# Layer-1 feed-forward, first pass: row statistics taken in the attention before it, normalization moved to ScalarE's tanh and VectorE, weight preparation cut into pieces

## The chip, the cores and the metric

The kernel runs on one core of a Trainium2 chip. Its engines are TensorE (PE; its weight loads are listed as PEld), VectorE (DVE), ScalarE (ACT), GpSimd (POOL) and the queue that issues most DMAs (SP). The metric is the device time of one execution in microseconds.

## The reference

Two layers, each a graph attention and a feed-forward, on 2708 rows of 256 values, in float32. What the change touches is the end of the second attention and the second feed-forward:

```python
def _L1_gnn_ref(x, adj_matrix, attn_mask, Wqkv, bqkv, Wout, bout, graph_bias):
    ...
    attn = jax.nn.softmax(scores, axis=-1)
    out = jnp.einsum('hnm,hmd->hnd', attn, vh)
    out = out.transpose(1, 0, 2).reshape(n, d)
    return out @ Wout + bout

def _L1_ffn_ref(x, ln_w, ln_b, W, b):
    def step(h, _):
        h = h + 0.01 * jnp.tanh(h)
        h = h * jax.nn.sigmoid(h)
        h = _layernorm(h, ln_w, ln_b)
        h = jnp.einsum('bsc,dc->bsd', h, W) + b
        return (h, None)
    x, _ = jax.lax.scan(step, x, None, length=30)
    return x
...
x = x + _L1_gnn_ref(_layernorm(x, axis=-1), adj, adj, ...)
x = x + _L1_ffn_ref((_layernorm(x, axis=-1))[None], ...)[0]
```

So the feed-forward starts with a layer norm of x (no weight, no bias), and then runs 30 iterations of blend, silu, layer norm and a 256x256 product.

## The kernel before

**Tiles and pairs.** The rows lie in 22 tiles of 128 (`NT`), two to a pair, so 11 pairs (`NPAIR`), in `X` of [128, 22, 256]. `BATCHES` groups the pairs for the small arithmetic on row statistics: pairs 0 to 2, 3 to 5, 6 to 8, and 9 to 10. Every stage is a `Phase` with a block in which each engine has its own program, written out by hand in order; semaphores join them, and a barrier of all engines ends the phase.

**Layer-1 attention** (`layer1_attention`, names `a_...`). Its steps run per tile (i, b) and pair of heads hp. In each such step PE turns the exponentials of two heads in three chunks c, DVE and ACT copy the turned blocks out of PSUM (L1075), DVE adds the bias and takes maxima of scores of later heads (L1160, L1165), ACT takes exponentials of later heads (L1124), and PE multiplies with V (L1301). In step hp = 0, chunk 1, `project` (L1206 on DVE) adds the projected output of the tile before to `X`; the last tile's stands alone at the end. POOL adds the adjacency bias (L1101) and the output bias to X (L1105), and has nothing more to do once the last tile's are done. The first and the last pair of tiles are written out, the nine between them are a hardware loop.

**Layer-1 feed-forward** (`layer1_ffn`, names `f_...`).

- *The first normalization.* DVE takes `bn_stats` of all 22 tiles of X in four hardware loops, with the moments of each batch behind them (`slot_moments`, L143 and L94 to L101). POOL turns each batch's moments into an inverse deviation and a shift (`slot_deviation`, `inverse_deviation`, L109 to L114: add, multiply, power, multiply), then writes the normalized rows to `gg` (`standard_rows`, L119), one instruction per tile.
- *The weights.* Four DMAs bring W, its bias, ln_w and ln_b. PE turns W (L2192), ACT copies it out (L2143), DVE scales it and makes two helper matrices (L2080 to L2084), PE multiplies these (L2198, L2202), DVE folds the biases and the mean in (L2088 to L2093). The products wait for that by `c_done`.
- *An iteration on a pair g.* ACT: tanh (L2118), from `gg` in the first pass, later from the product in PSUM. DVE: blend, 0.01 * tanh + h into `gg` (L2024). ACT: silu (L2122) into `th`. DVE: two `bn_stats` (L2031), and at a batch's last pair the moments. POOL: deviation of the batch (L109 to L114), then the standard rows `yy`, two instructions per pair (L119). PE: turn of `yy` (L2157). ACT: copy `f_yt` (L2108). PE: product (L2174).
- *Order.* DVE does in each pass blend g, then the statistics of g - 2. ACT does, for each g, the copy of turned g, tanh of g - 3, silu of g - 4. PE does turn g, then product g - 3; so the first product stands behind the turn of pair 3. The 30 iterations run one into the other.
- *Banks.* `RING` = 4 PSUM banks are shared by the pairs. Before product g PE waits until the bank's last user was blended, in the first pass too, where the blend reads `gg` and not the bank:

```python
if here and isinstance(i, int) and i == ITERS:
    pe.wait_ge(out_done, q + 1)
elif here:
    pe.wait_ge(g_done[q], i + 1)
else:
    pe.wait_ge(g_done[q], i)
```

For g = 0, 1, 2 of the first pass q is 8, 9, 10. Below, product 0 and product 1 are those of pairs 0 and 1 in the first pass.

## Time and profile before

| What | us |
|---|---|
| median of 3 runs | 2705.55 (2704.66 to 2706.4) |
| the profiled execution: time | 2703.6 |
| the profiled execution: span | 2701.8 |
| layer-1 attention, last operation (DVE, L1206) ends | 1925.83 in the span |
| first product of the feed-forward starts | 1967.45 in the span |

Over the whole span PE is busy for 92%, DVE for 74%, ACT for 60% and POOL for 53%. A timeline lists merged instructions of an engine with start and duration in us; "x6" says that six follow each other, and the brackets say how long the engine stood idle before them and what released it. Durations of neighbours overlap a little, so the time from one start to the next is often less than a duration.

### The profile page before, as it was taken

The numbers are of one execution on the slowest core, as the hardware profiler recorded it, in microseconds if no ns is written. First come the engines' busy times: TensorE is split into PE (matmuls) and PEld (weight loads), VectorE is DVE, ScalarE is ACT, GpSimd is POOL, SyncE is SP. The second block draws the span as 40 slices with busy tenths as digits, with TensorE's granted clock in tenths as the row PEclk, the third lists the DMA queues.
The fourth block names the chain that finished last, engine by engine and source line by source line (L and its number), as shares of the span: only waits on it lengthen the run. The fifth ranks groups of instructions, "written<-read, shape, count | busy, mean of one in ns | idle before, by whom it ended". The sixth has DMA issues, their size and how long they took to land. (4 is left out here: it accounts for less than half of the span.)

```text
span 2701.8 us, 58198 instructions
## 1 busy us (share of the span) xinstructions
PE 2479.9 (92%) x20186; PEld 2029.4 (75%) x20187; DVE 2001.9 (74%) x4248; ACT 1611.9 (60%) x3039; POOL 1419.9 (53%) x1728
## 2 busy tenths in 40 slices
PE   6799999999976997188999999999599999999999
PEld 5377777777765997166777777777478888888888
DVE  5899999999925443887777777777667777777776
ACT  1577777777721332245666666666467777777775
POOL 6366676667342553522112211111388888888886
PEclk9799999999967999599999999999799999999999
DMA  2011111111063223201111111110000000000001
GB/s 100 21 43 44 62 42 43 52 54 43 22 221 137 70 70 94 102 7 42 43 41 41 41 42 60 42 41 21 7 1 0 0 0 0 0 0 0 0 0 41
DMA packets 43862, 114.01 MB, mean 42 GB/s; under 512 B 5621, under 2 KB 29918, under 8 KB 37982
## 3 DMA queue, kind: packets, MB, share of 16 engines
q1 hardware_dynamic: 38174, 97.16, 10.2%
q0 software_dynamic: 5568, 15.21, 1.8%
q8 instruction: 80, 1.31, 0.2%
q14 instruction: 40, 0.33, 0.0%
HBM read 99.21 MB, written 13.15 MB: 42 GB/s over the span
## 5 line engine op out<-in xcount | busy, mean ns | idle before, releaser
L2174 PE MATMUL f_pm<-f_wl,f_yt 128*128 128x256 f32 x2640 | 624.9, 380 | 0.0
L2174 PEld LDWEIGHTS f_pm<-f_wl,f_yt 128*128 128x128 f32 x2640 | 476.9, 191 | 51.5
L1101 POOL TENSOR_TENSOR ADJ<-ADJ,a_off 128x2708 f32<-128x2708 f32 x22 | 131.3, 5967 | 542.8 <-DVE ADJ L1180 542.8
L119 POOL TENSOR_SCALAR f_yy<-f_th,f_rs 128x255 f32<-128x255 f32 x660 | 367.9, 573 | 21.8 <-POOL f_rs L114 21.8
L2024 DVE SCALAR_TENSOR_TENSOR f_gg<-f_th,f_pm 128x512 f32<-128x512 f32 x319 | 218.9, 686 | 177.4 <-ACT f_th L2118 177.2
L529 ACT COPY a_wt<-a_tp 128x512 f32<-128x512 f32 x528 | 256.5, 566 | 146.7 <-PE a_tp L744 146.6
L552 POOL TENSOR_SCALAR a_off<-ADJ 128x677 bf16<-128x677 f32 x84 | 284.3, 3407 | 76.2 <-DMA ADJ<-in_adj 61.8
L629 DVE SCALAR_TENSOR_TENSOR a_lg<-a_f1s,F2S,a_fo 128x1024 f32<-128x1024 f32 (+1 forms) x264 | 296.4, 1151 | 29.4 <-PE a_fo L731 28.1
L1160 DVE CUSTOM_DVE_ANT_0 a_sc<-a_qk,ADJ 128x1024 f32<-128x1024 f32 (+1 forms) x264 | 288.1, 1092 | 31.0 <-PE a_qk L1258 30.7
L2118 ACT ACTIVATE f_th<-f_pm 128x512 f32<-128x512 f32 x319 | 190.6, 597 | 200.3 <-PE f_pm L2174 200.3
L1124 ACT ACTIVATE a_sc<-a_sc,a_mx 128x1024 f32<-128x1024 f32 (+1 forms) x264 | 277.7, 1052 | 45.1 <-DVE a_mx L1165 45.1
L1075 ACT COPY a_wt<-a_tp 128x512 f32<-128x512 f32 x264 | 154.2, 584 | 236.1 <-PE a_tp L1280 235.3
L637 DVE CUSTOM_DVE_ANT_0 a_lg<-a_lg,ADJ 128x2708 f32<-128x2708 f32 x88 | 261.4, 2970 | 1.3 <-DVE a_lg L629 0.2
L1280 PE MATMUL a_tp<-ident,a_sc 128*128 128x128 f32 x1936 | 261.7, 276 | 0.2
L1280 PEld LDWEIGHTS a_tp<-ident,a_sc 128*128 128x128 f32 x1936 | 215.5, 141 | 42.2 <-issue 19.4
L744 PE MATMUL a_tp<-ident,a_lg 128*128 128x128 f32 x1936 | 245.3, 275 | 0.6 <-ACT a_wt L529 0.6
L2031 DVE BATCH_NORM_STATS2 f_st<-f_th 128x6 f32<-128x256 f32 x660 | 245.7, 414 | 0.0
L1301 PE MATMUL a_po<-a_wt,V 128*64 128x128 f32 x3872 | 240.3, 276 | 0.0
L1301 PEld LDWEIGHTS a_po<-a_wt,V 128*64 128x64 f32 x3872 | 208.7, 137 | 41.5 <-issue 36.3
L1075 DVE COPY a_wt<-a_tp 128x512 f32<-128x512 f32 (+1 forms) x264 | 158.2, 599 | 107.9 <-PE a_tp L1280 107.9
L759 PEld LDWEIGHTS a_po<-a_wt,V 128*64 128x64 f32 x3872 | 209.6, 137 | 37.1 <-issue 35.5
L576 ACT ACTIVATE a_lg<-a_lg,a_mx 128x2708 f32<-128x2708 f32 x88 | 226.5, 2574 | 11.9 <-DVE a_mx L640 11.4
(308 smaller groups left out, 4535.0 us busy)
## 6 DMA issues: line engine op xcount, KB each, us to landing
ADJ<-in_adj SPq DMA_DIRECT2D x44, 1354.0 KB, 5.8
W<-in_L_ffn_w SPq DMA_DIRECT2D x32, 512.0 KB, 9.3
m_got<-YD SPq DMA_DIRECT2D x6, 768.0 KB, 10.6
out<-X SPq DMA_DIRECT2D x21, 128.0 KB
X<-in_x SPq DMA_DIRECT2D x3, 768.0 KB, 10.2
XD<-XF SPq DMA_DIRECT2D x3, 768.0 KB
m_b<-in_L_ffn_b SPq DMA_DIRECT2D x1, 2048.0 KB, 7.8
m_rows<-XD,SLOT POOLq DMA_INDIRECT x58, 2.8
```

The lines of the kernel that those rows point to most:

```text
L119: return eng.tensor_scalar(out, x, rs[:, 0, bass.ds(t, 1)], rs[:, 1, bass.ds(t, 1)], ALU.mult, ALU.add)
L529: copy(wt[:, h // 2, h % 2, j:end, :], tp[:, BANKS[g], 0:(end - j) * P]).then_inc(copied[BANKS[g]], 1)
L552: pool.tensor_scalar(off[:, b, cols], adj[:, b, cols], 0.0, HUGE, ALU.is_equal, ALU.mult).then_inc(off_done[b], 1)
L629: dve.scalar_tensor_tensor(lg[:, unit.turn, c0:c0 + cn], f1s[:, h, c0:c0 + cn], F2S[:, bass.ds(i * 2 + b, 1), h], fo[:, s, 0:cn], ALU.add, ...
L637: dve.tensor_tensor_reduce(lg[:, unit.turn, :], lg[:, unit.turn, :], adj[:, b, :], 1.0, FLOOR, ALU.mult, ALU.max, mx[:, h, 0:1]).then_inc( ...
L1075: copy(wt[:, (hp * NC + c) % 2, s, j - c * CT:end - c * CT, :], tp[:, bank(group), 0:(end - j) * P]).then_inc(copied[bank(group)], 1)
L1124: act.activation(sc[:, h, c0:c0 + cn], sc[:, h, c0:c0 + cn], ACT.Exp, bias=mx[:, h, NC:NC + 1], accum_out=den[:, h, c:c + 1]).then_inc(exp ...
L1160: dve.tensor_tensor_reduce(sc[:, h, c0:c0 + cn], qk[:, s, 0:cn], adj[:, b, c0:c0 + cn], 1.0, -BIG, ALU.add, ALU.max, mx[:, h, c:c + 1]).th ...
L1280: mm = pe.transpose(tp[:, bank(group), (j - j0) * P:(j - j0 + 1) * P], sc[:, h, col:col + P], ident[:, :])
L1301: mm = pe.matmul(po[s * HD:(s + 1) * HD, 0:P], V[:, j, 2 * hp + s, 0:HD], wt[:, (hp * NC + c) % 2, s, j - c * CT, :], start=(j == 0), stop ...
L2031: dve.bn_stats(st[:, 2 * g + r, :], th[:, g, r, :]).then_inc(stat_done[g], 1)
L2174: mm = pe.matmul(out, yt[:, g, r, k, :], wl[:, k, :], start=(k == 0), stop=(k == KD - 1))
```

## The change

`bn_stats` of X moves out of the feed-forward into the attention: DVE takes it for a tile one chunk after the tile's projection was added, and for the last tile at the attention's very end. In the attention's pair 10, tile 0, DVE also folds the moments of the first 18 tiles (`READY`), and POOL makes their inverse deviation behind its last bias. Three buffers (`ST`, `MOM`, `RS`) are kept from one phase to the other. The feed-forward begins with the moments of the last four tiles on DVE and their deviation on POOL. POOL writes no normalized rows any more. ACT's first tanh reads X with RS as scale and bias, one instruction for each tile. DVE writes the normalized rows to `gg` a batch at a time, then blends the batch, then takes its statistics; the weight work is cut into three pieces behind blend 0, blend 1 and the first batch's statistics. ACT's copy of the turned weights moves behind silu 0.

```diff
+READY = 2 * BATCHES[-1][0]
...
 def layer1_attention(nc, io, keep, layer1):
-    X, V, ident = keep["X"], keep["V"], keep["ident"]
+    X, V, ident, neg_half, st, mom, rs = (keep[n] for n in ("X", "V", "ident", "neg_half", "ST", "MOM", "RS"))
...
                 for b in range(2):
                     bias(i, b)
                     residual(i, b)
+            pool.wait_ge(x_moments, 1)
+            inverse_deviation(pool, mom, rs, neg_half, 0, READY, x_pchain, 0)
...
+            def statistics(i, b, k):
+
+                dve.wait_ge(copied[k], uses(*later((i, b, 0), H)[:2], ("project",)) if later((i, b, 0), H)
+                            else 2 * ROUNDS * NPAIR + 1)
+                t = i * 2 + b
+                dve.bn_stats(st[:, bass.ds(t, 1), :], X[:, bass.ds(t, 1), :]).then_inc(x_stats, 1)
...
                         reciprocals(i, b, hp)
+                    if c == 2 and hp == 0 and later(unit, -H):
+                        statistics(*later(unit, -H)[:2], bank(("project",)))
+                        if isinstance(i, int) and i == NPAIR - 1 and b == 0:
+                            dve.wait_ge(x_stats, READY)
+                            row_moments(dve, st, mom, 0, READY, x_folded, 0).then_inc(x_moments, 1)
...
             project(NPAIR - 1, 1, 0)
+            statistics(NPAIR - 1, 1, 0)
...
@@ layer1_ffn, gpsimd
-            for g in range(NPAIR):
-                slot_deviation(pool, 2 * g, mom, rs, neg_half, x_moments, x_pchain, x_inv)
-                for r in range(2):
-                    standard_rows(pool, gg[:, g, r:r + 1, :], X[:, 2 * g + r:2 * g + r + 1, :], rs,
-                                  2 * g + r).then_inc(h_done, 1)
+            pool.wait_ge(x_moments, 1)
+            inverse_deviation(pool, x_mom, x_rs, neg_half, READY, NT, x_pchain, 0).then_inc(x_inv, 1)
...
@@ layer1_ffn, vector: weights(0), weights(1), weights(2) hold the lines that stood here in one piece
-            slot_moments(dve, X, st, mom, x_stats, x_folded, x_moments)
...
-            elementwise_dve(dve, 0)
+            row_moments(dve, x_st, x_mom, READY, NT, x_folded, 0).then_inc(x_moments, 1)
+            for k, (a, z) in enumerate(BATCHES):
+                if 2 * a == READY:
+                    dve.wait_ge(x_inv, 1)
+                for q in range(2 * a, 2 * z):
+                    standard_rows(dve, gg[:, q // 2, q % 2:q % 2 + 1, :], X[:, q:q + 1, :], x_rs, q).then_inc(h_done, 1)
+                dve.wait_ge(h_done, 2 * z)
+                for g in range(a, z):
+                    blend(dve, 0, g)
+                    if k == 0 and g < a + 2:
+                        weights(g - a)
+                for g in range(a, z):
+                    if g < NPAIR - 2:
+                        stats(dve, 0, g)
+                if k == 0:
+                    weights(2)
...
@@ layer1_ffn, scalar
         def tanh(act, i, g):
             if isinstance(i, int) and i == 0:
-                act.wait_ge(h_done, 2 * g + 2)
-                src = gg[:, g, :, :]
+                if 2 * g == READY:
+                    act.wait_ge(x_inv, 1)
+                for r in range(2):
+                    q = 2 * g + r
+                    op = act.activation(th[:, g, r, :], X[:, q, :], ACT.Tanh, scale=x_rs[:, 0, q:q + 1],
+                                        bias=x_rs[:, 1, q:q + 1])
+                op.then_inc(tanh_done[g], 1)
...
                     if not (isinstance(i, int) and i == ITERS):
                         silu(act, i, g - LAG - 1)
+                    if isinstance(i, int) and i == 0 and g == LAG + 1:
+                        act.wait_ge(w_ps, 1)
+                        act.copy(wt[:, :, :, :], pt[:, 0, :]).then_inc(w_sb, 1)
...
         @block.scalar
         def _(act):
-            act.wait_ge(w_ps, 1)
-            act.copy(wt[:, :, :, :], pt[:, 0, :]).then_inc(w_sb, 1)
             act_stream(act, 0)
```

How the instructions stand now. The changed kernel has the same lines under somewhat higher numbers (L1075 is L1079, L2024 is L2043).

DVE in the attention, pair 10 and tile 0, second half of the first head pair, before:

```order
L1206 TENSOR_TENSOR X<-a_tp,X 128x256
L1186 TENSOR_REDUCE a_tot<-a_den 128x2
L1188 RECIPROCAL a_tot<-a_tot 128x2
L1190 COPY a_spread<-a_tot 128x128
L1075 COPY a_wt<-a_tp 128x256
L1160 ISA a_sc,a_mx<-a_qk,ADJ 128x1024
L1160 ISA a_mx 128x1
L1075 COPY a_wt<-a_tp 128x256
L1160 ISA a_sc,a_mx<-a_qk,ADJ 128x660
L1160 ISA a_mx 128x1
L1165 TENSOR_REDUCE a_mx<-a_mx 128x1
L1075 COPY a_wt<-a_tp 128x512
```

and with the change:

```order
L1079 COPY a_wt<-a_tp 128x256
L1166 ISA a_sc,a_mx<-a_qk,ADJ 128x660
L1166 ISA a_mx 128x1
L1171 TENSOR_REDUCE a_mx<-a_mx 128x1
L1219 BN_STATS ST<-X 128x6
L94 TENSOR_TENSOR MOM<-ST 128x18
L95 TENSOR_TENSOR MOM<-ST 128x18
L96 TENSOR_TENSOR MOM<-ST 128x18
L98 SCALAR_TENSOR_TENSOR MOM<-MOM 128x18
L101 SCALAR_TENSOR_TENSOR MOM<-MOM 128x18
L1079 COPY a_wt<-a_tp 128x512
L1166 ISA a_sc,a_mx<-a_qk,ADJ 128x1024
```

The statistics of the tile before, and here the moments of 18 columns, stand between the last maximum of the first head pair and the first copy of the second.

DVE at the beginning of the feed-forward, before (`f_lbc`, `f_last` and `f_wl` are weight matrices, `f_gg` the blend's input and output, `f_th` tanh and silu):

```order
L2080 TENSOR_SCALAR f_lbc<-f_ones,f_lnwb 128x128 x2
L2081 TENSOR_SCALAR f_last<-f_ones,ident 128x128
L2084 TENSOR_SCALAR f_wl<-f_wt,f_lnwb 128x256 x2
L2088 TENSOR_TENSOR f_call<-f_pm,f_bb 128x256
L2091 TENSOR_TENSOR f_wl<-f_wl,f_pm 128x256 x2
L2093 SCALAR_TENSOR_TENSOR f_wl<-f_call,ident,f_wl 128x256
L2024 SCALAR_TENSOR_TENSOR f_gg<-f_th,f_gg 128x512 x3
L2031 BN_STATS f_st<-f_th 128x6 x2
L2024 SCALAR_TENSOR_TENSOR f_gg<-f_th,f_gg 128x512
L2031 BN_STATS f_st<-f_th 128x6 x2
L2024 SCALAR_TENSOR_TENSOR f_gg<-f_th,f_gg 128x512
L2031 BN_STATS f_st<-f_th 128x6 x2
```

and with the change:

```order
L94 TENSOR_TENSOR MOM<-ST 128x4
L95 TENSOR_TENSOR MOM<-ST 128x4
L96 TENSOR_TENSOR MOM<-ST 128x4
L98 SCALAR_TENSOR_TENSOR MOM<-MOM 128x4
L101 SCALAR_TENSOR_TENSOR MOM<-MOM 128x4
L119 TENSOR_SCALAR f_gg<-X,RS 128x256 x6
L2043 SCALAR_TENSOR_TENSOR f_gg<-f_th,f_gg 128x512
L2098 TENSOR_SCALAR f_lbc<-f_ones,f_lnwb 128x128 x2
L2100 TENSOR_SCALAR f_last<-f_ones,ident 128x128
L2043 SCALAR_TENSOR_TENSOR f_gg<-f_th,f_gg 128x512
L2104 TENSOR_SCALAR f_wl<-f_wt,f_lnwb 128x256 x2
L2043 SCALAR_TENSOR_TENSOR f_gg<-f_th,f_gg 128x512
```

The normalization of a batch comes to DVE, and the weight work stands between the blends instead of ahead of them.

ACT at the same place, before:

```order
L2143 COPY f_wt<-f_pt 128x512
L2118 ACTIVATE f_th<-f_gg 128x512 x2
L2122 ACT_TABLE_LOAD
L2122 ACTIVATE f_th<-f_gg 128x512
L2118 ACTIVATE f_th<-f_gg 128x512
L2122 ACTIVATE f_th<-f_gg 128x512
L2118 ACTIVATE f_th<-f_gg 128x512
L2122 ACTIVATE f_th<-f_gg 128x512
```

and with the change:

```order
L2151 ACTIVATE f_th<-X,RS 128x256 x4
L2161 ACT_TABLE_LOAD
L2161 ACTIVATE f_th<-f_gg 128x512
L2178 COPY f_wt<-f_pt 128x512
L2151 ACTIVATE f_th<-X,RS 128x256 x2
L2161 ACTIVATE f_th<-f_gg 128x512
L2151 ACTIVATE f_th<-X,RS 128x256 x2
L2161 ACTIVATE f_th<-f_gg 128x512
```

Every tanh of the pass is two instructions on X, and the copy of the turned weights stands behind the first silu.

## Rows read from the trace of the kernel before

**Rows 1.** Busy time by stage; columns: stretch, length, then each engine's busy microseconds.

```profile
1250.00:1940.00 690.00, 670.77 (x6812) 521.32 (x6810) 527.41 (x1107) 420.73 (x806) 140.86 (x56) 0.99 0.11 39
2020.00:2700.00 680.00, 674.58 (x3666) 579.49 (x3664) 487.73 (x1451) 476.55 (x898) 548.32 (x1044) 1.00 0.01 4
```

**Rows 2.** Timeline of PE; columns: start, duration, engine, line, operation, count, idle before.

```profile
1931.13 1.12 PE L2192 MATMUL f_pt<-ident,f_wn 128*128 128x128 f32 x4 [5.76 <-DMA f_lnwb<-in_L_ffn_ln_b]
...
1960.03 3.23 PE L2157 MATMUL f_pt<-ident,f_yy 128*128 128x128 f32 x12 [13.24 <-POOL f_yy L119]
1966.54 1.12 PE L2157 MATMUL f_pt<-ident,f_yy 128*128 128x128 f32 x4 [3.28 <-POOL f_yy L119]
1967.45 2.81 PE L2174 MATMUL f_pm<-f_wl,f_yt 128*128 128x256 f32 x8
...
1970.54 1.89 PE L2174 MATMUL f_pm<-f_wl,f_yt 128*128 128x256 f32 x8
```

**Rows 3.** Timeline of POOL, feed-forward's first pass.

```profile
1934.41 3.28 POOL L119 TENSOR_SCALAR f_gg<-X,f_rs 128x256 f32<-128x256 f32 x6
...
1946.07 4.97 POOL L119 TENSOR_SCALAR f_gg<-X,f_rs 128x256 f32<-128x256 f32 x6
...
1956.11 0.25 POOL L109 TENSOR_SCALAR f_rs<-f_mom 128x6 f32<-128x6 f32 x1
...
1958.73 3.36 POOL L119 TENSOR_SCALAR f_yy<-f_th,f_rs 128x255 f32<-128x255 f32 x6 [0.18 <-POOL f_rs L114]
```

**Rows 4.** Timeline of DVE, end of the attention and first feed-forward instruction.

```profile
1883.38 0.69 DVE L1075 COPY a_wt<-a_tp 128x512 f32<-128x512 f32 x1 [1.53 <-PE a_tp L1280]
...
1898.57 0.69 DVE L1075 COPY a_wt<-a_tp 128x512 f32<-128x512 f32 x1 [1.53 <-PE a_tp L1280]
...
1925.41 0.42 DVE L1206 TENSOR_TENSOR X<-a_tp,X 128x256 f32<-128x256 f32 x1 [1.28 <-PE a_tp L1311]
1927.14 0.43 DVE L143 BATCH_NORM_STATS2 f_st<-X  x1 [1.30 <-PEq L58]
```

**Rows 5.** Timeline of DVE, feed-forward's first and second pass.

```profile
1943.87 0.60 DVE L2084 TENSOR_SCALAR f_wl<-f_wt,f_lnwb 128x256 f32<-128x256 f32 x2
...
1946.83 0.75 DVE L2091 TENSOR_TENSOR f_wl<-f_wl,f_pm 128x256 f32<-128x256 f32 x2 [0.43 <-PE f_pm L2202]
1947.62 0.48 DVE L2093 SCALAR_TENSOR_TENSOR f_wl<-f_call,ident,f_wl 128x256 f32<-128x256 f32 x1
1948.02 1.57 DVE L2024 SCALAR_TENSOR_TENSOR f_gg<-f_th,f_gg 128x512 f32<-128x512 f32 x2
...
1951.78 0.74 DVE L2031 BATCH_NORM_STATS2 f_st<-f_th 128x6 f32<-128x256 f32 x2
1952.44 0.67 DVE L2024 SCALAR_TENSOR_TENSOR f_gg<-f_th,f_gg 128x512 f32<-128x512 f32 x1
1953.04 0.74 DVE L2031 BATCH_NORM_STATS2 f_st<-f_th 128x6 f32<-128x256 f32 x2
...
1954.92 0.68 DVE L2024 SCALAR_TENSOR_TENSOR f_gg<-f_th,f_gg 128x512 f32<-128x512 f32 x1
...
1973.70 0.75 DVE L2031 BATCH_NORM_STATS2 f_st<-f_th 128x6 f32<-128x256 f32 x2
...
1975.26 0.69 DVE L2024 SCALAR_TENSOR_TENSOR f_gg<-f_th,f_pm 128x512 f32<-128x512 f32 x1
```

**Rows 6.** Timeline of ACT, feed-forward's first pass.

```profile
1932.28 0.59 ACT L2143 COPY f_wt<-f_pt 128x512 f32<-128x512 f32 x1 [11.40 <-PE f_pt L2192]
...
1937.30 1.28 ACT L2122 ACT_TABLE_LOAD   x1
...
1950.31 0.61 ACT L2118 ACTIVATE f_th<-f_gg 128x512 f32<-128x512 f32 x1
```

**Rows 7.** Timeline of DVE in the expert stage: the same helper as POOL's normalization.

```profile
766.56 3.40 DVE L119 TENSOR_SCALAR XF<-X,GW 128x256 f32<-128x256 f32 x10
```

**Rows 8.** Timeline of ACT in the expert stage: 256 columns, scale and bias from memory.

```profile
1087.69 2.08 ACT L1907 ACTIVATE m_z<-XF,m_rs 128x256 f32<-128x256 f32 x4 [24.85 <-POOL m_rs L114]
```

More of the change, by code:

```diff
@@ L1957, in layer1_ffn @@
 def layer1_ffn(nc, io, keep):
-    X, ident, neg_half = (keep[n] for n in ("X", "ident", "neg_half"))
+    X, ident, neg_half, x_st, x_mom, x_rs = (keep[n] for n in ("X", "ident", "neg_half", "ST", "MOM", "RS"))
     with Phase(nc, "f1") as ph:
@@ L2096, in _, with weights @@
-            elementwise_dve(dve, 0)
+            def weights(piece):
+                if piece == 0:
+                    dve.wait_ge(w_in, 64)
+                    dve.wait_ge(ones_done, 2)
+                    for k in range(KD):
+                        dve.tensor_scalar(lbc[:, k, :], ones[:, :], lnwb[:, 1, k:k + 1], None,
+                                          ALU.mult).then_inc(w_scaled, 1)
+                    dve.tensor_scalar(last[:, :], ones[:, :], ident[:, P - 1:P], None, ALU.mult).then_inc(w_scaled, 1)
+                elif piece == 1:
+                    dve.wait_ge(w_sb, 1)
+                    for k in range(KD):
+                        dve.tensor_scalar(wl[:, k, :], wt[:, k, :, :].rearrange("p j o -> p (j o)"),
+                                          lnwb[:, 0, k:k + 1], None, ALU.mult).then_inc(w_scaled, 1)
+                else:
+                    dve.wait_ge(c_mm, 1)
+                    dve.tensor_tensor(call[:, :], pm[:, 0, 0:D], bb[:, :], ALU.add).then_inc(cchain, 1)
+                    dve.wait_ge(last_mm, 1)
+                    for k in range(KD):
+                        dve.tensor_tensor(wl[:, k, :], wl[:, k, :], pm[:, 1, 0:D], ALU.subtract).then_inc(cchain, 1)
+                    dve.wait_ge(cchain, 1 + KD)
+                    dve.scalar_tensor_tensor(wl[:, KD - 1, :], call[:, :], ident[:, P - 1:P], wl[:, KD - 1, :], ALU.mult,
+                                             ALU.add).then_inc(c_done, 1)
@@ L2244, in build @@
         early.close()
-        with ExitStack() as part:
-            layer1 = buffers(part, V1=([P, NT, H, VW],), QT=([P, H, NT * P], F16), KH=([P, H, N], F16),
-                             KL=([P, H, N], F16), ADJ1=([P, 2, N],))
-            layer1["adj_in"] = adj_in[2:]
-            layer1_prepare(nc, io, {**keep, "V": layer1["V1"]}, layer1)
-            layer1_attention(nc, io, {**keep, "V": layer1["V1"]}, layer1)
-        layer1_ffn(nc, io, keep)
+        with ExitStack() as rest:
+            keep.update(buffers(rest, ST=([P, NT, 6],), MOM=([P, 5, NT],), RS=([P, 4, NT],)))
+            with ExitStack() as part:
+                layer1 = buffers(part, V1=([P, NT, H, VW],), QT=([P, H, NT * P], F16), KH=([P, H, N], F16),
+                                 KL=([P, H, N], F16), ADJ1=([P, 2, N],))
+                layer1["adj_in"] = adj_in[2:]
+                layer1_prepare(nc, io, {**keep, "V": layer1["V1"]}, layer1)
+                layer1_attention(nc, io, {**keep, "V": layer1["V1"]}, layer1)
+            layer1_ffn(nc, io, keep)
 _INS = ["x", "adj", "L0_gnn_weight", "L0_gnn_weight_u", "L0_gnn_weight_v", "L0_gnn_bias", "L0_gnn_proj_w",
```

25 lines of the change are left out of this document (4 added, 21 removed).

## The prediction

> **What bounds the kernel now.** I read the busy time by stage first, then each engine's timeline around the start of the feed-forward. In its thirty iterations PE is busy for 674.6 of 680 us at the full clock, and in the layer-1 attention for 670.8 of 690 us [rows 1]. Both stages belong to PE: work on other engines there is free while it stays in their idle time, and nothing in the loop can absorb a change in when it begins. Between them lies a stretch in which PE hardly works: weight turns at 1931.13, the first turns of an iteration at 1960.03, the fourth at 1966.54 after 3.28 us of waiting for POOL, the first product at 1967.45, the second at 1970.54 [rows 2]. From the second product PE is never short of work for long, so the time of **product 1** (the second) carries the change: what it gains, the end gains.
>
> Before, that stretch is POOL's: it normalizes 22 tiles of X, six in 3.28 us when alone and in 4.97 us beside DVE, then starts the deviation of the first batch at 1956.11 and its y rows at 1958.73 [rows 3]. That is one inverse deviation in 2.62 us, and six y rows in 3.36.
>
> The sum below is made in this execution's clock (span 2701.8 us, time 2703.6); the median of the three runs is 2705.55, 1.95 higher. I take the difference in us off the median.
>
> **Part 1: statistics in the attention.** It adds 22 BN_STATS to DVE, 0.43 us each [rows 4], 21 of them behind the last score of a tile's first head pair. DVE then waits 1.53 us for PE before its next copy; I found 1.52 to 1.54 us at all twenty such places, one of the loop and the last one before the tail standing in [rows 4]. With some 0.08 for the wait's own instruction, 0.51 fits: cost 0. At tile 20 the moments of 18 columns come on top, five tiny operations with two waits. From the end of a statistics pair to the operation behind such moments it takes 1.56 - 0.75 = 0.8 to 1.88 - 0.74 = 1.1 us [rows 5], so 0.43 + 0.8 to 1.1 = 1.2 to 1.6 against 1.53: at most 0.1 out, taken as 0. POOL's deviation of 18 columns runs some 25 us before the stage ends, beside a free POOL. If the cover were gone everywhere, 22 x 0.51 + 1 = 12.2 us would be added: 0 and 12.2 are the bounds, and the measured gap puts it at 0. The 22nd stands uncovered behind the last addition to X (1925.41), where all wait for DVE at the stage's barrier: +0.53 with its wait on its own result. So everything in the feed-forward starts 0.53 later, DVE at 1927.67 instead of 1927.14 [rows 4], and PE's weight turns at 1931.66, still released by the loads.
>
> **Part 2: the new first pass.** DVE now normalizes, ACT computes tanh from X itself, POOL only does y. Durations: DVE normalization by the same helper, ten in 3.40, so 0.33 each [rows 7]; blend 0.60 to the next operation, a pair of statistics 0.66, a pair with moments behind it and on to the next operation 1.56 to 1.88, I take 1.70 [rows 5]. On ACT the 128x512 tanh takes 0.61 [rows 6]; one of 256 columns with scale and bias from memory has no row, but the Identity of that form has: four in 2.08, 0.60 for the last, so 0.49 from one to the next and 1.09 for a split tanh [rows 8]. Successive ACT operations overlap by about a tenth: 0.52 for a silu, 0.48 for a copy of 0.59.
> The Trainium skill, "ScalarE: Activation LUTs", section "What ACT_TABLE_LOAD costs", gives 186 ns plus 0.833 ns per element, and 93 ns for each pointer operand; by it a half would be an estimated 585 ns, and the trace's Identity agrees.
>
> The walk, each step released by the last one to come:
> Start to batch 0. Moments of the last four columns and six normalizations are done by about 1930.5, the table load of 1.28 us [rows 6] lies beside them, blend 0 ends at 1931.3. Then the weights' path is later than DVE: turns 1931.66 + 1.12, copy to 1933.40, and tanh 2 stands behind that copy: 1933.30 + 1.09 = 1934.39. The first two pieces of weight work (0.60 for two full-size scalings, the first piece less) fit in DVE's waits before that. Blend 2 to 1935.04, two pairs of statistics to 1936.36, the third waits for silu 2 (ACT did tanh 3 first) till 1936.45 and with the moments ends at 1938.15.
> Batch 1. Third piece of weight work 0.42 + 0.75 + 0.48 less overlaps, 1.55; six normalizations and a wait, 2.15: 1941.85. Blends 3 and 4 to 1943.06; blend 5 waits for silu 3 and tanh 5 on ACT, 1942.57 + 0.52 + 1.09 = 1944.19; it and two pairs to 1946.16; silu 5, then statistics and moments to 1947.95.
> Batch 2. 2.15 to 1950.1, blends 6 and 7 to 1951.3. Blend 8 waits for ACT: silu 6, a copy of turned y, tanh 8, 1950.83 + 0.52 + 0.46 + 1.09 = 1952.9; two pairs of statistics to 1954.9; silu 8 behind silu 7, a copy and tanh 9, 1955.4; then 1.70: 1957.1.
> Batch 3. Four normalizations and a wait 1.5, blend 9 of 0.69: 1959.3.
> **What is late next:** product 0 needs turn 3, thus y of batch 1: 1948 + 2.62 + 1.1 = 1951.7, and blend 8 (1953.6). Product 1 needs blend 9, the last user of its bank by the generic wait, though the first pass doesn't use that bank. So product 1 starts at 1959.3 instead of 1970.54: **-11.2 us**. POOL then keeps up: y of batch 2 from 1957.1 + 2.62 + 0.6 = 1960.3, the turn that wants it stands behind products 1 and 2, two spans of about 2 us from 1959.3, at about 1963.
>
> **Corrections.** PE is idle for about 2 us before product 1 and hardly worked before. Before, the turns behind 3.28 us of idleness took 1.12 for four, and product 0 2.81 against 1.89 for product 1 [rows 2]. Bounds 0 (clock kept) and 1.7 (all of product 1 and its turn at the lower of the two levels); half, +0.8, since product 0 lies shortly before. Contention: six blends with both inputs in SBUF now lie beside POOL's y rows; a pair of blends took 1.57 instead of 1.29 beside POOL [rows 5], and only part is on the path: bounds 0 and 3, taken +0.8. Sum: -11.2 + 0.8 + 0.8 = **-9.6**, so 2705.55 - 9.6 = **2695.9 us**.
>
> **Rivals.**
> *Contended.* Beside DVE POOL's six rows went from 3.28 to 4.97 [rows 3]; if DVE pays as POOL did, six blends wait half a POOL row (0.28) to a whole one (0.56), 1.7 to 3.4, and each of four moment groups 0.3 more: +3 instead of 0.8, with the cold product +0.9 more. Against it: DVE's other blends there show 0.67 to 0.68. It gives -6.5: 2699.
> The Trainium skill, "SBUF — State Buffer", section "SBUF: two separate sides", says that a DVE operation with two SBUF inputs and a GpSimd operation that reads SBUF lock each other out for a whole instruction. By that rule each of the six blends may wait for a whole POOL row; the rows above show such waits at some places only.
> *Better.* Moments at 1.56, normalization at the 0.27 pitch of the scalings (0.60 for two), no cold product, no contention: -0.4 - 1 - 1.6 more, 2693 or a little under.
> *Statistics on PE's path.* If the next copy were late at every tile, part 1's 12.2 eats the gain: 2708. The 1.53 us gap speaks against it.
> *Slower.* One mechanism: statistics read X just after the addition in the loop, and DVE drains for it. It decides where a tile's added time passes 1.53 us; to lose 5.4 us net, 21 x (d - 1.53) must reach 15, d = 2.25 us. At d = 2.5 it is 20.4 - 9.6 = +10.8: 2716. The nearest, an in-loop BN_STATS on another stage's row, has 0.43 [rows 4].
> *The change doesn't do what it says:* product 1 is held by something not seen, such as DVE's first batch waiting longer for weights; 5 us more gives 2701.
>
> **How the numbers follow.** Forecast (2693 to 2698) 0.62; contended 0.17; held by something else 0.08; better 0.06; statistics on the path 0.04; slower 0.03. The range leaves out the last two and the edges: low end, all bounds at their best, about -13.5; high end, contention 3, cold 1.7, long moments 0.5 give -6, and two more for what isn't seen, -4. So 2692 to 2701.5. A measurement tells 0.2%, 5.4 us, from no change. Faster by that (under 2700.1): forecast, better, most of contended, a part of held, 0.84; within: 0.13; slower: 0.03.
>
> **What would show it.** DVE's gap before the first copy of a head pair shrinks from 1.53 to about 1.0, and PE's rows in the attention keep their pace. The barrier comes 0.5 later. POOL's first y row at about 1941 and idle before it. The split tanh with about 1.09. Product 0 near 1953.6, product 1 right behind blend 9, near 1959.3 to 1960. From there to the end the same time as before. Wrong would be: a longer attention, product 1 held by POOL's y, halves of tanh at other prices, or a loop that runs slower than before.

## The result, and the profile after

The changed kernel takes 2692.29 us (median of 5 runs, 2691.5 to 2692.86) beside 2705.28 us for the kernel before (5 runs, 2704.66 to 2706.4): a ratio of 0.995 with a 95% interval of 0.9938 to 0.9962, so 13.0 us less. In a later comparison it took 2692.28 beside 2704.99. The prediction was -9.6, to 2695.9. Its direction and place were right, its size was 3.4 us short. The profiled run took 2692.86 us, its span is 2690.9. One run of kernel 5 below, 3343.0 us at a mean granted clock of 0.736, was a slow one and is left out of its median.

Because two executions of one program are shifted against each other long before the changed code (the attention's first addition to X lies between 1272.9 and 1277.9 us in fourteen profiles), times of before and after are compared here from the last addition to X on: 1925.41 before [rows 4], 1926.48 after. What is 1.07 later than before is at the same time.

By stage (columns: stretch, length, busy microseconds of PE, PEld, DVE, ACT and POOL with instruction counts, granted clock, DMA share, GB/s), the loop's stretch set 10 us earlier than in [rows 1]:

```profile
1250.00:1940.00 690.00, 674.83 (x6827) 524.19 (x6825) 536.77 (x1135) 427.43 (x819) 140.76 (x53) 0.99 0.11 39
2010.00:2690.00 680.00, 673.72 (x3662) 578.75 (x3660) 487.23 (x1450) 476.12 (x896) 547.78 (x1042) 1.00 0.01 4
```

Both stages are PE's as before. The attention from its first to its last addition to X takes 651.81 us, before 651.79; from product 1 to the end of the span it is 731.30, before 731.26. The whole difference lies between. PE's timeline there (columns: start, duration, engine, line, operation, count, idle before and its releaser), to be held against [rows 2]:

```profile
1932.61 1.12 PE L2232 MATMUL f_pt<-ident,f_wn 128*128 128x128 f32 x4 [6.17 <-DMA f_lnwb<-in_L_ffn_ln_b]
...
1944.32 2.13 PE L2197 MATMUL f_pt<-ident,f_yy 128*128 128x128 f32 x8 [6.99 <-POOL f_yy L119]
...
1952.88 1.12 PE L2197 MATMUL f_pt<-ident,f_yy 128*128 128x128 f32 x4 [4.91 <-POOL f_yy L119]
1954.23 3.65 PE L2214 MATMUL f_pm<-f_wl,f_yt 128*128 128x256 f32 x8 [0.23 <-DVE f_gg L2043]
1957.72 0.60 PE L2197 MATMUL f_pt<-ident,f_yy 128*128 128x128 f32 x4
1959.60 1.97 PE L2214 MATMUL f_pm<-f_wl,f_yt 128*128 128x256 f32 x8 [1.28 <-DVE f_gg L2043]
```

Product 1 is the row at 1959.60, released by blend 9 on DVE as forecast. Less 1.07 it is 1958.53, 12.0 us before the 1970.54 of [rows 2]. POOL's timeline shows the idle time that took the place of its 22 normalizations [rows 3], and y rows that take 5.14 and 4.08 us for six where six alone take 3.33:

```profile
1939.10 0.26 POOL L109 TENSOR_SCALAR f_rs<-f_mom 128x6 f32<-128x6 f32 x1 [7.32 <-DVE f_mom L101]
...
1941.66 5.14 POOL L119 TENSOR_SCALAR f_yy<-f_th,f_rs 128x255 f32<-128x255 f32 x6 [0.19 <-POOL f_rs L114]
...
1951.46 4.08 POOL L119 TENSOR_SCALAR f_yy<-f_th,f_rs 128x255 f32<-128x255 f32 x6 [0.18 <-POOL f_rs L114]
...
1960.29 3.33 POOL L119 TENSOR_SCALAR f_yy<-f_th,f_rs 128x255 f32<-128x255 f32 x6 [0.18 <-POOL f_rs L114]
```

DVE's timeline: a statistics instruction with the next copy in the attention's loop, the one at tile 20 (moments of 18 columns lie behind it), then the path of the first pass:

```profile
1438.37 0.43 DVE L1219 BATCH_NORM_STATS2 ST<-X  x1
1439.91 0.69 DVE L1079 COPY a_wt<-a_tp 128x512 f32<-128x512 f32 x1 [1.12 <-PE a_tp L1299]
...
1882.83 0.42 DVE L1219 BATCH_NORM_STATS2 ST<-X 128x6 f32<-128x256 f32 x1
...
1884.45 0.69 DVE L1079 COPY a_wt<-a_tp 128x512 f32<-128x512 f32 x1 [0.58 <-PE a_tp L1299]
...
1928.97 2.03 DVE L119 TENSOR_SCALAR f_gg<-X,RS 128x256 f32<-128x256 f32 x6
...
1938.85 0.42 DVE L2108 TENSOR_TENSOR f_call<-f_pm,f_bb 128x256 f32<-128x256 f32 x1
...
1942.42 1.38 DVE L2043 SCALAR_TENSOR_TENSOR f_gg<-f_th,f_gg 128x512 f32<-128x512 f32 x2
1944.89 0.92 DVE L2043 SCALAR_TENSOR_TENSOR f_gg<-f_th,f_gg 128x512 f32<-128x512 f32 x1 [1.08 <-ACT f_th L2151]
...
1948.47 2.02 DVE L119 TENSOR_SCALAR f_gg<-X,RS 128x256 f32<-128x256 f32 x6
...
1953.38 0.70 DVE L2043 SCALAR_TENSOR_TENSOR f_gg<-f_th,f_gg 128x512 f32<-128x512 f32 x1 [1.56 <-ACT f_th L2151]
...
1955.89 0.75 DVE L2050 BATCH_NORM_STATS2 f_st<-f_th 128x6 f32<-128x256 f32 x2 [0.49 <-ACT f_th L2161]
...
1957.35 1.38 DVE L119 TENSOR_SCALAR f_gg<-X,RS 128x256 f32<-128x256 f32 x4
1958.76 1.29 DVE L2043 SCALAR_TENSOR_TENSOR f_gg<-f_th,f_gg 128x512 f32<-128x512 f32 x2
```

The waits named with ACT are the three of the walk: blend 5 for silu 3 and tanh 5, blend 8 for silu 6, a copy and tanh 8, the last statistics of batch 2 for silu 8. On ACT a split tanh takes 1.09 and the table load 1.28, as taken:

```profile
1930.49 1.28 ACT L2161 ACT_TABLE_LOAD   x1
...
1934.25 1.09 ACT L2151 ACTIVATE f_th<-X,RS 128x256 f32<-128x256 f32 x2
```

### The profile page after: what moved, and what is told of

It is laid out like the page before. It is cut to its first block and busy times, and to the rows that moved or that the text cites. A ratio compares the mean times of both kernels' runs of the same rounds, so it can differ in the third digit from the quotient of the medians.

```text
span 2690.9 us, 58121 instructions
## 1 busy us (share of the span) xinstructions
PE 2480.2 (92%) x20186; PEld 2029.6 (75%) x20187; DVE 2005.5 (75%) x4260; ACT 1617.1 (60%) x3050; POOL 1405.8 (52%) x1698
## 5 line engine op out<-in xcount | busy, mean ns | idle before, releaser
L2043 DVE SCALAR_TENSOR_TENSOR f_gg<-f_th,f_pm 128x512 f32<-128x512 f32 x319 | 219.0, 687 | 174.2 <-ACT f_th L2157 173.8
L1079 ACT COPY a_wt<-a_tp 128x512 f32<-128x512 f32 x264 | 154.3, 584 | 236.1 <-PE a_tp L1299 235.4
L1079 DVE COPY a_wt<-a_tp 128x512 f32<-128x512 f32 (+1 forms) x264 | 158.4, 600 | 98.8 <-PE a_tp L1299 98.8
```

The source lines that it names most:

```text
L1079: copy(wt[:, (hp * NC + c) % 2, s, j - c * CT:end - c * CT, :], tp[:, bank(group), 0:(end - j) * P]).then_inc(copied[bank(group)], 1)
```

## The experiments

All are compared with the kernel before by runs on the same chip (before: 2705.44 us for kernels 1 to 4, 2704.63 for 5 to 8, 2704.99 for 9 to 11 and the repetition). Since their difference to each other is small, each is also read in its profile, by the time of **product 3** after the attention's first addition to X: at the fourth product PE is at full speed and nearly all waits of the start are behind it. From there to the end of the span it is 725.1 to 727.3 us in the fourteen profiles. No edit touches the loop there, so these 2 us, like the 5 us between the earliest and the latest first addition, are mostly spread between executions; a median of four or five runs carries them too, and product 3 does not.

| Kernel | Median, us | Ratio (95%) | Product 3, us |
|---|---|---|---|
| before | 2705.3 | 1 | 701.25 |
| after | 2692.29 | 0.995 (0.9938 to 0.9962) | 689.33 |
| after, again | 2692.28 | 0.9956 (0.9942 to 0.9969) | 689.26 |
| 1 no bank wait | 2690.51 | 0.9947 (0.993 to 0.9963) | 687.33 |
| 2 statistics moved only | 2693.41 | 0.9959 (0.9945 to 0.9973) | 691.38 |
| 3 weight work in one piece | 2696.55 | 0.9968 (0.9956 to 0.9981) | 693.51 |
| 4 statistics back | 2704.97 | 1.0 (0.9991 to 1.001) | 702.24 |
| 5 statistics three times | 2691.72 | 0.9955 (0.9939 to 0.997) | 689.88 |
| 6 statistics six times | 2694.18 | 0.9961 (0.9947 to 0.9975) | 692.09 |
| 7 batch 1 on POOL | 2688.84 | 0.994 (0.9923 to 0.9957) | 688.69 |
| 8 batches 1 and 2, no bank wait | 2687.59 | 0.9935 (0.9918 to 0.9952) | 685.05 |
| 9 batch 1, no bank wait | 2688.37 | 0.9938 (0.9922 to 0.9953) | 684.97 |
| 10 POOL filled | 2692.87 | 0.9957 (0.9942 to 0.9972) | 690.81 |
| 11 as 8, whole tanh | 2687.27 | 0.9933 (0.9918 to 0.9949) | 686.14 |

**After, again.** The changed kernel unaltered.

> The changed kernel once more, unchanged, beside the others: how far its time and its profile repeat. Its first median was 13.0 us under that of before, while product 1 moved by 12.0 against the first addition of the attention. If the missing 1.0 is spread between executions, this median lies anywhere in 2691.5 to 2694 and product 3 again 689.3 +- 0.4 after the first addition; if it is real, 2692.3 +- 0.5 and a stretch outside the two is shorter again.

Product 3 repeats within 0.07 us and the median within 0.01. The median is again 12.7 us under before, while product 3 moved by 12.0. The median fits both expectations; product 3 and the stretches fit the first, since none after the first addition to X is shorter. What 1 us more is, lies ahead of it or in the spread of the single profiled runs (before's took 2703.6, 1.7 under its median; after's 0.6 over its own). The profiles can't tell which.

### Which part of the change earns the gain

**2, statistics moved only.** Normalization goes back to POOL, tanh to one instruction from its output, the weight work to one piece ahead of the first blend and ACT's copy of the turned weights ahead of its first tanh.

```diff
             inverse_deviation(pool, x_mom, x_rs, neg_half, READY, NT, x_pchain, 0).then_inc(x_inv, 1)
+            pool.wait_ge(x_inv, 1)
+            for g in range(NPAIR):
+                for r in range(2):
+                    standard_rows(pool, gg[:, g, r:r + 1, :], X[:, 2 * g + r:2 * g + r + 1, :], x_rs,
+                                  2 * g + r).then_inc(h_done, 1)
...
-                for r in range(2):
-                    q = 2 * g + r
-                    op = act.activation(th[:, g, r, :], X[:, q, :], ACT.Tanh, scale=x_rs[:, 0, q:q + 1],
-                                        bias=x_rs[:, 1, q:q + 1])
-                op.then_inc(tanh_done[g], 1)
+                act.wait_ge(h_done, 2 * g + 2)
+                act.activation(th[:, g, :, :], gg[:, g, :, :], ACT.Tanh).then_inc(tanh_done[g], 1)
...
```

> The statistics and their moments stay in the attention, everything else in the feed-forward is as before: POOL normalizes all 22 tiles, tanh reads gg in one instruction, the weight work stands in one piece ahead of the blends. Theory A (the statistics ahead of POOL were what made its chain late): POOL normalizes from 1931.8 on, 22 x 0.56 = 12.3 us alone and up to 16 beside DVE, then a deviation of 2.6: first y rows at 47 to 50 instead of 1958.73, product 1 near 1960 to 1962, thus 9 to 11 us below before, nearly all of the gain. Theory B (taking the normalization off POOL is what pays): no more than half of the gain, 4 to 6 us below before.

**4, statistics back.** The reverse: tanh from X, normalization on DVE and weight work in pieces stay; statistics, moments and deviations return to the feed-forward.

```diff
-            row_moments(dve, x_st, x_mom, READY, NT, x_folded, 0).then_inc(x_moments, 1)
+            slot_moments(dve, X, x_st, x_mom, x_stats, x_folded, x_moments)
             for k, (a, z) in enumerate(BATCHES):
-                if 2 * a == READY:
-                    dve.wait_ge(x_inv, 1)
+                dve.wait_ge(x_inv, k + 1)
...
-            statistics(NPAIR - 1, 1, 0)
```

> The changed kernel with the statistics of all 22 tiles back at the start of the feed-forward, in the four hardware loops of before with a deviation per batch; the attention is that of before. Theory A: normalization on DVE then starts near 1943.8 instead of 1928.97, 14.9 us later; the waits for the loads and the weights of about 2 us vanish, so product 1 comes 13 us later and the time is that of before within 2 us. Theory B (the move of the normalization is worth something by itself): 4 us or more below before.

Kernel 2 keeps 9.9 of the 11.9 us at product 3; kernel 4 loses all of it and 1.0 more (the median is that of before). Theory A holds in both. The two halves of the change are not a sum: all that was reordered in the feed-forward together is worth 2.0 with the statistics already moved, and nothing without. Kernel 4's DVE timeline says why: the statistics of the 22 tiles, in the path in groups like this one, hold the first normalization until 1943.24, where after's began at 1928.97 (the last addition to X lies within 0.04 us in both):

```profile
1933.30 2.91 DVE L143 BATCH_NORM_STATS2 ST<-X  x6
...
1943.24 2.02 DVE L119 TENSOR_SCALAR f_gg<-X,RS 128x256 f32<-128x256 f32 x6
```

And kernel 2's POOL timeline shows that POOL, started at once and never waiting, does all 22 normalizations (0.67 each beside DVE) and reaches its first y row at 1949.51, before at 1958.73 [rows 3]:

```profile
1931.03 14.63 POOL L119 TENSOR_SCALAR f_gg<-X,RS 128x256 f32<-128x256 f32 x22
...
1949.51 3.33 POOL L119 TENSOR_SCALAR f_yy<-f_th,f_rs 128x255 f32<-128x255 f32 x6 [0.19 <-POOL f_rs L114]
```

**3, weight work in one piece.** All three pieces stand ahead of the first blend again, and ACT's copy of the turned weights first on its queue.

```diff
                 dve.wait_ge(h_done, 2 * z)
+                if k == 0:
+                    for piece in range(3):
+                        weights(piece)
                 for g in range(a, z):
                     blend(dve, 0, g)
-                    if k == 0 and g < a + 2:
-                        weights(g - a)
...
-                    if isinstance(i, int) and i == 0 and g == LAG + 1:
-                        act.wait_ge(w_ps, 1)
-                        act.copy(wt[:, :, :, :], pt[:, 0, :]).then_inc(w_sb, 1)
...
```

> The changed kernel with the three pieces of weight work together ahead of blend 0, and ACT's copy of the turned weights ahead of its first tanh, as before. Theory A (the pieces hide the waits for the loads and for PE): blend 0 waits for piece 3 until about 1938.3 instead of 1931.03, the moments of batch 0 come 4 to 5 us later, batch 1's normalization 3.5 us later since piece 3 is then done, product 1 3 to 3.5 us later: 9.5 to 10 us below before. Theory B (DVE's later waits for ACT absorb it): under 1 us above the changed kernel.

It costs 4.2 us at product 3 and 4.3 in the median, 0.7 more than its theory A's upper figure. DVE's timeline: the first piece starts after 1.80 us of idleness for which the profile names no releaser, and the others wait for the round trip over ACT or PE, with nothing to do meanwhile.

```profile
1935.21 0.48 DVE L2098 TENSOR_SCALAR f_lbc<-f_ones,f_lnwb 128x128 f32<-128x128 f32 x2 [1.80 <-issue]
...
1936.94 0.62 DVE L2104 TENSOR_SCALAR f_wl<-f_wt,f_lnwb 128x256 f32<-128x256 f32 x2 [1.05 <-ACT f_wt L2181]
1939.07 0.42 DVE L2108 TENSOR_TENSOR f_call<-f_pm,f_bb 128x256 f32<-128x256 f32 x1 [1.51 <-PE f_pm L2236]
1939.92 0.75 DVE L2111 TENSOR_TENSOR f_wl<-f_wl,f_pm 128x256 f32<-128x256 f32 x2 [0.43 <-PE f_pm L2240]
```

Kernels 2 and 3 both have the statistics in the attention and the weight work in one piece; they differ in who normalizes, what tanh reads, and the order of blends and statistics that goes with it. With POOL as before product 3 comes at 691.38 (kernel 2), with DVE and the split tanh at 693.51 (kernel 3). Normalization on DVE with all that belongs to it is thus 2.1 us worse without the weight work in pieces, and pays only with it, by the 4.2 that the pieces are worth. The intervals of the two medians overlap; the 2.1 are read from one profile each.

### How much cover the attention has

Kernels 5 and 6 repeat each statistics instruction into a spare buffer, kernel 5 twice more, kernel 6 five times more.

```diff
                 dve.bn_stats(st[:, bass.ds(t, 1), :], X[:, bass.ds(t, 1), :]).then_inc(x_stats, 1)
+                for k2 in range(5):
+                    dve.bn_stats(spare[:, k2, :], X[:, bass.ds(t, 1), :])
```

> The changed kernel with every BN_STATS in the attention issued three times instead of once (the two more write to a buffer that nobody reads). In the changed kernel DVE still waits 1.18 us for PE behind the statistics of a tile (0.58 at the tile that also folds 18 columns). Two more at 0.34 each are 0.68. Theory A (the gap is cover, and only what passes it counts): 0 in the loop, 0.1 at that one tile, 0.68 at the uncovered last one: 0.8 us above the changed kernel. Theory B (each statistics on DVE delays PE, the first one too): 22 x 0.68 = 15 us above.

> The changed kernel with every BN_STATS in the attention issued six times: five more at 0.34 are 1.70 us, 0.52 past the 1.18 us that DVE waits for PE. Theory A (what passes the gap delays PE one to one): 20 x 0.52 + 1.1 at the tile with the moments + 1.7 at the last = 13.2 us above the changed kernel. Theory C (the copies have slack of their own behind the gap, a bank deep): 2 to 5 us above.

With three, product 3 is 0.55 later (theory A). The attention is 651.75 us long with three, and 652.95 with six: +1.1 for 105 instructions of 0.34. Five more take 1.71 us per tile, over the 1.12 us that the first left of the gap, and yet PE loses 0.05 a tile. Kernel 6 at tile 20, where the moments come on top:

```profile
1884.26 0.42 DVE L1220 BATCH_NORM_STATS2 ST<-X 128x6 f32<-128x256 f32 x1
1884.59 1.71 DVE L1222 BATCH_NORM_STATS2 a_spare<-X 128x6 f32<-128x256 f32 x5
...
1886.85 0.68 DVE L1080 COPY a_wt<-a_tp 128x512 f32<-128x512 f32 x1
1887.45 1.21 DVE L1167 CUSTOM_DVE_ANT_0 a_sc<-a_qk,ADJ 128x1024 f32<-128x1024 f32 x1
```

The copy has no idle time before it, so it is late, and the work behind it follows without a wait until DVE has caught up. The gap before a copy is thus not the whole slack; behind it lie other gaps (0.27 to 0.72 us in kernel 5's rows of the same stretch). That is theory C of kernel 6, and its 2 to 5 us hold the +2.8 at product 3. Of these only 1.1 is passed on by late copies; the rest, 1.6, is five uncovered instructions behind the last tile.

### What holds product 1, and PE's clock

**1, no bank wait.** In the first pass the products don't wait for blends that use no PSUM bank.

```diff
             elif here:
                 pe.wait_ge(g_done[q], i + 1)
-            else:
+            elif some(i - 1):
                 pe.wait_ge(g_done[q], i)
```

> The changed kernel, but in the first pass products 0, 1 and 2 no longer wait for the blend of the bank's last user (blends 8, 9, 10), which does not read the bank in that pass. In the changed kernel product 0 starts at 1954.23 behind blend 8 and product 1 at 1959.60 after 1.28 us of waiting for blend 9. Theory A (product 1 carries the change, what it gains the end gains): product 1 goes to about 1957.9, 1.7 us earlier, and the time falls by 1.7 us below the changed kernel. Theory B (ACT and DVE are equally late there): turn 0 of the second iteration, which waited 0.37 us for POOL at 1974.92, hangs on tanh 2 of the second pass, and ACT, busy without a gap from silu 9 at 1959.48 to 1963.6, can't give that more than 0.2 us earlier; PE then waits there for 1.5 us more, and the time falls by 0.2 us at most.

```profile
1952.62 3.33 PE L2214 MATMUL f_pm<-f_wl,f_yt 128*128 128x256 f32 x8
1955.79 0.60 PE L2197 MATMUL f_pt<-ident,f_yy 128*128 128x128 f32 x4
1956.22 1.89 PE L2214 MATMUL f_pm<-f_wl,f_yt 128*128 128x256 f32 x8
```

In PE's timeline product 1 follows without a gap, and product 3 comes 2.0 us earlier, as its theory A has it. The median gains 1.8, which the intervals of the ratios can't tell from nothing.

**7, batch 1 on POOL,** in POOL's idle time before its first y rows; DVE waits for it. **8** does so for batches 1 and 2, with the edit of kernel 1; **9** for batch 1 with that edit; **11** is 8 with one tanh instruction for each of pairs 3 to 8, from what POOL wrote.

```diff
             inverse_deviation(pool, x_mom, x_rs, neg_half, READY, NT, x_pchain, 0).then_inc(x_inv, 1)
+            for k in [1]:
+                for q in range(2 * BATCHES[k][0], 2 * BATCHES[k][1]):
+                    standard_rows(pool, gg[:, q // 2, q % 2:q % 2 + 1, :], X[:, q:q + 1, :], x_rs, q).then_inc(gp_done, 1)
...
+                if k in by_pool:
+                    dve.wait_ge(gp_done, 6 * (by_pool.index(k) + 1))
...
```

> The changed kernel with batch 1's six normalizations moved from DVE back to POOL, into the 7.32 us in which POOL waits for the first moments (6 x 0.56 = 3.4 us). Theory A (the first pass is DVE's and ACT's chain, product 1 carries it): DVE is 2.0 us earlier from batch 1 on, ACT's waits move along, product 1 2.0 us earlier: 2 us below the changed kernel. Theory B (ACT is late as soon as DVE is earlier): tanh 5, tanh 8 and silu 8 hold DVE back, under 1 us.

> The changed kernel with the normalizations of batches 1 and 2 on POOL (12 x 0.56 = 6.7 us of the 7.32 free, more beside DVE) and without the first pass's wait for the bank's last user. If both are additive: DVE 4.0 us earlier by batch 2, POOL's first deviation up to 1.5 us later; 3 to 4 us below the changed kernel, 2688 to 2689. If ACT's chain is the next bound: 1 to 2 us below it.

> POOL normalizes batch 1, and product 1 no longer waits for blend 9 in the first pass. It separates the two edits of the run in which POOL took batches 1 and 2. Theory A (the wait for blend 9 was all that was left behind an early product 0): product 1 follows product 0 without a gap and at 1.9 to 2.1 us, the cold product of 3.58 us goes, and product 3 comes 685.0 to 686.0 us after the attention's first addition to X, about 2688 in time. Theory B (batch 2's six normalizations on DVE hold the next turns): product 3 at 686.5 or more, 2689.5.

```diff
+                if batch_of(g) in (1, 2):
+                    act.wait_ge(gp_done, 2 * (g - BATCHES[1][0]) + 2)
+                    op = act.activation(th[:, g, :, :], gg[:, g, :, :], ACT.Tanh)
...
```

> POOL normalizes batches 1 and 2, product 1 doesn't wait for blend 9, and the tanh of pairs 3 to 8 is one instruction of 512 columns that reads what POOL wrote, instead of two halves that read X. It tests the price of the split on the path: DVE waited 1.08 and 1.56 us for ACT at blends 5 and 8 in the run without this edit. Theory A (ACT is late there by its own work, silu, a copy and a tanh in a row): 0.48 less per tanh, both waits shrink by about 0.5, product 3 comes 684.0 to 684.6 us after the attention's first addition instead of 685.05, time 2686.5 to 2687.3. Theory B (ACT now waits for POOL's rows, 0.65 each beside DVE): tanh 3 and 4 come later, no gain or up to 1 us lost, 2687.5 to 2688.5.

Kernel 7 is the run in which the feared cold product happens. Its product 1 comes earlier as theory A has it, but only 0.6 us of that are left at product 3. Kernel 8 gains 4.3 there, somewhat more than if both its edits were additive, and kernel 9 gains 4.4, its theory A. PE's timeline, then its busy stretches of kernel 7 (the last four columns: POOL, granted clock, DMA share, GB/s):

```profile
1955.15 3.02 PE L2221 MATMUL f_pm<-f_wl,f_yt 128*128 128x256 f32 x8 [0.23 <-DVE f_gg L2043]
1958.00 0.60 PE L2204 MATMUL f_pt<-ident,f_yy 128*128 128x128 f32 x4
1960.51 3.58 PE L2221 MATMUL f_pm<-f_wl,f_yt 128*128 128x256 f32 x8 [1.91 <-DVE f_gg L2043]
```

```profile
1960.50:1964.00 3.50, 3.49 (x9) 2.68 (x10) 1.82 (x4) 2.49 (x5) 3.24 (x8) 0.53 0.00 0
```

Its product 1 starts 2.3 us earlier than after's (682.60 against 684.93 from the first addition), behind 1.91 us of waiting for blend 9, and runs at a granted clock of 0.53, the lower of the two levels, in 3.58 us; product 2 is only 0.6 earlier. After's own product 1, behind 1.28 us, ran at the full clock:

```profile
1954.20:1957.70 3.50, 3.47 (x8) 2.76 (x9) 2.84 (x13) 3.12 (x7) 1.46 (x4) 0.51 0.00 0
1959.60:1961.50 1.90, 1.90 (x9) 1.64 (x10) 0.83 (x2) 1.90 (x5) 1.64 (x5) 1.00 0.00 0
```

Without the wait for blend 9 the loss is gone (kernel 9: product 0 in 2.90, product 1 right behind it in 1.89), and product 3 comes 3.7 us earlier, though the medians differ by only 0.5. Kernel 7's profile is of the slowest of its four runs (2694.17, the others 2687.82 to 2689.40), and 3.2 us of that lie ahead of the attention's first addition (1277.91, after's 1274.67). How often its product 1 was cold is therefore not shown. Taking batch 2 off DVE as well changed nothing that is seen at product 3 (8 against 9: 0.08). Kernel 9's product 1 comes even 0.7 earlier than kernel 8's, but turn 6, ahead of product 3, then waits for POOL's y: once the wait for blend 9 is gone, what product 1 gains is no longer all gained at the end.

```profile
1959.25 0.66 PE L2204 MATMUL f_pt<-ident,f_yy 128*128 128x128 f32 x4 [0.45 <-POOL f_yy L119]
```

Kernel 11 shortened DVE's waits for ACT from 1.08 to 0.61 and from 1.56 to 1.10, as its theory A had it, but product 0 came only 0.3 earlier and took 3.62 where kernel 8's took 2.83: product 3 is 1.1 later, which neither of its theories had, and the median the same within the error. How much of product 0 falls at the lower clock differs between executions of one kernel too (3.65 and 3.24 for after), so differences under a microsecond can't be judged here.

**10, POOL filled.** POOL makes 18 rows that nobody reads in its idle time.

```diff
+            for n in range(18):
+                standard_rows(pool, spare[:, n:n + 1, :], X[:, n:n + 1, :], x_rs, n)
             elementwise_pool(pool, 0)
```

> POOL makes 18 rows that nobody reads, right behind the deviation of the last four tiles, into buffers of their own: 6 to 12 us of POOL beside DVE's six normalizations, the first three blends, nine statistics and the weight work, where POOL was idle before (from 1932 to 1939). It prices what a busy POOL costs DVE. Theory A (POOL pays, DVE hardly): DVE's groups in that stretch lengthen by less than 0.5 us together, the 18 rows take 0.5 to 0.65 each where DVE works, the first deviation of the loop starts up to 3 us later, which turn 0 only sees, and product 1 moves by -0.2 to +0.5: time 2692 to 2693. Theory B (DVE pays half a row to a row for each of its big instructions, as the prediction's contended rival says): three blends, six normalizations, three full scalings and nine statistics, 0.15 to 0.4 each where they meet: DVE 2 to 5 us later at the end of batch 0, product 1 +1.5 to +4, time 2694 to 2696.

DVE's timeline (where after has 0.17 at L98 and L101, 0.48 at the third piece's last, 2.02 for six):

```profile
1937.20 0.42 DVE L98 SCALAR_TENSOR_TENSOR f_mom<-f_mom 128x6 f32<-128x6 f32 x1
1937.65 0.51 DVE L101 SCALAR_TENSOR_TENSOR f_mom<-f_mom 128x6 f32<-128x6 f32 x1
...
1939.19 0.85 DVE L2116 SCALAR_TENSOR_TENSOR f_wl<-f_call,ident,f_wl 128x256 f32<-128x256 f32 x1
1939.96 2.76 DVE L119 TENSOR_SCALAR f_gg<-X,RS 128x256 f32<-128x256 f32 x6
```

and POOL's:

```profile
1930.35 11.26 POOL L119 TENSOR_SCALAR f_spare<-X,RS 128x256 f32<-128x256 f32 x18
```

With a POOL that is busy throughout, product 3 is 1.5 us later: the low edge of theory B, and more than A allowed. The loss sits in the moments (0.25 + 0.34), the last of the weight work (0.37) and six normalizations (0.74), together 1.7. The two blends beside the same rows took 0.70 and 0.69 as ever, and six statistics 2.17 as in after. So theory B's size came, but of the instructions it named only the normalizations paid; blends, scalings of 256 columns and statistics did not, and the moments, which it left out, did. The median says 0.6 more than after's repetition, too little to be told from it.

The Trainium skill, "SBUF — State Buffer", section "SBUF: two separate sides", gives the port that DVE and GpSimd share to whichever comes first, for a whole instruction, against DVE operations with two SBUF inputs and also those in a mode that reads through both ports; the small operations with two SBUF inputs, longer by 0.25 and 0.34, agree with it, and the two blends at an unchanged 0.70 don't show it. Whether the normalizations, longer by 0.12 each, run in such a mode no run here shows.

## Where the prediction held, and the step that failed

Right were the place (product 1, held by blend 9), the direction and the mechanism: what the rows had as POOL's path became DVE's, and nothing before or behind moved. Step by step, times of after less 1.07 us:

| Step | Forecast | Measured |
|---|---|---|
| Turns of the weights | 1931.66 | 1931.54 |
| Tanh 2 ends | 1934.39 | 1934.27 |
| Batch 0's moments end (next operation starts) | 1938.15 | 1937.78 |
| Blend 5 starts | 1944.2 | 1943.82 |
| Batch 1's moments end | 1947.95 | 1947.40 |
| Turn 3 | 1951.7 | 1951.81 |
| Product 0 | 1953.6 | 1953.16 |
| Blend 8 starts | 1952.9 | 1952.31 |
| Batch 2's moments end | 1957.1 | 1956.28 |
| Product 1 | 1959.3 | 1958.53 |

*Part 1* held. DVE's gap before the copy shrinks from 1.53 to 1.12 us (0.41, where 0.51 was taken), at tile 20 with the moments (0.70 to their end) to 0.58, and PE is still what it waits for; the stage is as long as before. At the barrier it cost less than the 0.53 taken: DVE's first operation behind it comes 1.93 us after the last addition, before 1.73, so 0.20. The turns of the weights, which the path takes next, come 0.41 later than before.

*Part 2's walk* came out 0.8 us too long. The term that was mis-sized is "a pair with moments behind it", 1.70 from a range of 1.56 to 1.88 [rows 5]: in the batches the last pair and the moments take 1.43 to 1.46, three times, so 0.7 in all. Six normalizations and a wait were taken as 2.15; the next blend starts 2.05 behind the first of them, in three batches 0.3. The turns gave 0.1. Contention, which the walk left out, is in the measured times and took 0.2 to 0.3 back.

*Corrections* is the step that failed most: it added 1.6 us where the runs show 0.3 to 0.4. The cold product was taken as +0.8 on product 1: it took 1.97 us instead of 1.89 and its successor came 2.24 instead of 2.16 later. The granted clock rose only at the end of product 0 (0.51 until 1957.7), which paid for it (3.65) in time that product 1 spent waiting anyway. The bound of 1.7 was right: kernel 7 shows it at 1.7 (3.93 from product 1 to 2 against 2.24). That it did not come here is in part luck: kernel 7 waited 0.6 us longer behind a product 0 of 3.02, and paid in full. The prediction's own sum, with about 2 us of idleness, lies nearer to kernel 7. Contention was taken as +0.8 on DVE. In the run POOL paid, 1.8 and 0.75 us for two batches of y, off the path, and DVE 0.09 on one pair of blends (1.38 for 1.29) and 0.23 on one blend (0.92 for 0.69), at most 0.3; kernel 10 shows 1.5 when POOL is busy from the start, half the bound of 3.

Together: the walk apart from contention 1.1, the cold product 0.7 (0.8 taken, 0.08 measured), contention 0.5 (0.8 taken, 0.3 measured). These 2.3 us are what lies between the -9.6 forecast and the -11.9 measured at product 3. The other 1.1 of the median's -13.0 is in no step and stays open, as said above.

The low end of the range, "all bounds at their best, about -13.5", is not the sum of its terms: -11.2 - 0.4 - 1 = -12.6, the figure of *better*. The 0.9 between has no source in the prediction.

Of the rivals, *better* came nearest: "2693 or a little under" is within 0.7 us of the measured time. Of its four conditions three happened (cheap moments, no cold product, hardly any contention); the normalization kept its 0.33. It had a chance of 0.06, as if each were luck of its own, while in this run the last two had one thing in common: who paid for them was off the path or waiting anyway. *Contended* had POOL's price right (4.97 for six, now 5.14) and put it on the wrong engine. The 3.28 us "when alone" that it starts from were not alone: DVE took statistics of X in that stretch, which thus cost POOL nothing seen. *Statistics on PE's path* and *slower* are excluded with room: 105 more statistics, 36 us at 0.34 each, lengthened the attention by 1.1.

## What to carry to other kernels

Look for work that can be done on each piece of data where it is produced, in a stage whose engine for it has gaps: the same 22 statistics that, with their moments and deviations, cost 12.9 us at a stage's start (kernel 4 against after) left the attention's length as it was inside the stage before and cost 0.2 at its end, and the reordering around them was worth nothing without that. Before a correction for contention or a lowered clock goes into the sum, name the operation that pays it and see whether it is on the path: here it mostly wasn't, in kernel 7 it was. And where a wait is generic (a bank that the first pass doesn't use), drop it in the pass that doesn't need it: kernels 8, 9 and 11, at 2687.3 to 2688.4 us, take it away and give POOL's idle time to the normalization, and stand some 4 to 5 us under the changed kernel in the median and 3.2 to 4.4 at product 3. The intervals of the ratios still touch.
